# Retention layers: the next tile's rows transposed behind the gate projection, the gate function ahead of their scaling

## The reference

```
xn = layer_norm(x, ln1_scale, ln1_bias)
q, k, v = xpos(xn @ wq), xpos(xn @ wk), xn @ wv
heads = (q @ k.T * decay) @ v
y = group_norm(heads) * gn_scale + gn_bias
tmp = xn @ Wg;  swish = tmp * sigmoid(tmp)
x = swish * y @ Wo + x
```

## Time and profile before

| | |
|---|---|
| Time of the kernel before, median of 3 | 1639.94 us (1636.73 to 1643.91) |
| Time of the profiled execution | 1640.97 us |
| Its span, first to last instruction | 1639.2 us |
| PE busy | 1600.9 us, 98% |
| DVE busy | 1003.4 us, 61% |
| ACT busy | 848.5 us, 52% |
| Eight retention tiles of layer 0 | about 535 to 663 us |
| Eight retention tiles of layer 1 | about 850 to 986 us |

### The profile page before, as it was taken

One profiled execution on the slowest core, in us unless ns is written; L12 is line 12 of the kernel. 1 busy time (PEld: TensorE's weight loads), 2 busy tenths in 40 slices (PEclk: granted clock), 3 DMA queues, 4 the chain that ended last, 5 costly groups with the idle time before them and its releaser, 6 DMA issues.

```text
span 1639.2 us, 31503 instructions
## 1 busy us (share of the span) xinstructions
PE 1600.9 (98%) x12078; PEld 1344.9 (82%) x12078; DVE 1003.4 (61%) x2002; ACT 848.5 (52%) x1195; POOL 420.9 (26%) x358
## 2 busy tenths in 40 slices
PE   9999999999998999999999999999979999999997
PEld 8888888888887788888877888878878888888886
DVE  5334444444446777643366767444559999999994
ACT  4454444454445433453343334534337888788883
POOL 1333333333332544100005444000022112112111
PEclk8999999999999999999999999999989999999999
DMA  5110111111202100223241002234251555536612
GB/s 203 40 40 28 39 39 39 30 34 39 77 26 94 70 2 1 78 92 101 90 149 53 2 1 90 91 116 138 106 206 26 180 179 165 206 102 234 211 22 71
DMA packets 35840, 143.77 MB, mean 88 GB/s; under 512 B 4977, under 2 KB 5361, under 8 KB 28529
## 3 DMA queue, kind: packets, MB, share of 16 engines
q1 hardware_dynamic: 30592, 130.65, 22.7%
q0 software_dynamic: 5168, 12.06, 3.6%
HBM read 222.39 MB, written 12.85 MB: 144 GB/s over the span
## 4 chain that ended last, share of the span: by engine, by line
PE 59%; DVE 4%; DMA 2%; ACT 1%; issue 1%; POOL 0%; SPq 0%; DVEq 0%; POOLq 0%; ACTq 0%
PE bank L99 36%; PE bank L1664 10%; PE bank L2139 7%; PE bank L1555 2%; PE bank L2145 2%; PE bank L1568 1%; DVE e_w L2066 1%; DMA A<-xh_d,token 1%; PE bank L1648 1%; DMA out<-acc_d 0%; PE bank L1683 0%; DMA wraw<-in_wa 0%; DMA acc_d<-A,token 0%; DVE X L1530 0%; DVE fw L1360 0%
## 5 line engine op out<-in xcount | busy, mean ns | idle before, releaser
L2066 DVE TENSOR_TENSOR e_w<-e_raw,e_w 128x2048 fp32r<-128x2048 f32 x134 | 302.2, 2281 | 19.6 <-ACT e_w L1948 19.1
L1948 ACT ACTIVATE e_w<-e_raw 128x2048 fp32r<-128x2048 f32 x134 | 256.8, 1918 | 36.8 <-PE bank L2139 17.7
L99 PE MATMUL bank<-e_w,e_xT 128*128 128x512 f32 x1104 | 271.4, 395 | 0.0
L99 PEld LDWEIGHTS bank<-e_w,e_xT 128*128 128x128 f32 x1104 | 204.0, 188 | 41.3
L99 PE MATMUL bank<-ctx,wk 128*128 128x258 f32 x1536 | 191.8, 284 | 0.0
L1664 PE MATMUL bank<-fw,hh 128*128 128x512 f32 x768 | 186.2, 392 | 2.7 <-DVE hh L1482 2.7
L99 PE MATMUL bank<-x2T,fw 128*128 128x512 f32 x768 | 186.7, 392 | 0.0
L99 PEld LDWEIGHTS bank<-ctx,wk 128*128 128x128 f32 x1536 | 186.4, 192 | 0.2
L1664 PEld LDWEIGHTS bank<-fw,hh 128*128 128x128 f32 x768 | 144.5, 189 | 33.7 <-issue 2.2
L99 PEld LDWEIGHTS bank<-x2T,fw 128*128 128x128 f32 x768 | 143.5, 188 | 29.7
L622 DVE TENSOR_SCALAR_CACHE_REDUCE u<-bank,thr 128x257 f32<-128x257 f32 x128 | 54.5, 481 | 169.4 <-PE bank L826 169.4
(11 more groups left out here) (257 smaller groups left out, 2560.1 us busy)
## 6 DMA issues: line engine op xcount, KB each, us to landing
e_raw<-in_we SPq DMA_DIRECT2D x138, 1024.0 KB, 5.4
fraw<-in_wf SPq DMA_DIRECT2D x64, 512.0 KB, 3.6
ctxraw<-in_ctx SPq DMA_DIRECT2D x32, 514.0 KB, 3.5
wraw<-in_wa SPq DMA_DIRECT2D x20, 512.0 KB, 4.4
X<-in_x SPq DMA_DIRECT2D x4, 512.0 KB, 7.0
acc_d<-X SPq DMA_DIRECT2D x8, 256.0 KB, 4.0
xh_d<-A SPq DMA_DIRECT2D x8, 256.0 KB, 3.1
out<-acc_d SPq DMA_DIRECT2D x4, 512.0 KB, 5.8
```

What stands on the lines that cost most here:

```text
L99: last = nc.tensor.matmul(out, lhs(t, a), rhs(t, b), start=start and n == 0, stop=n == len(steps) - 1)
L1948: nc.scalar.activation(w[pos][:, 0, :, :], raw[pos][:, :, :], ACT.Copy).then_inc(m["w_hi"], 1)
L2066: nc.vector.tensor_tensor(w[pos][:, 1, :, :], raw[pos][:, :, :], r(w[pos][:, 0, :, :]), ALU.subtract).then_inc(m["w_lo"], 1)
```

## The change

On both engines one step moves to a later place in the same tile; nothing is added or taken away. It holds for tiles 1 to 6 of both layers, twelve tiles in all. Tile 0 had an order of its own already and keeps it, and tile 7 has no next tile.

```
# ACT
-                            if not (begin or end):
-                                norm_hi(n + 1, 1 - k)
                             act.wait_ge(m["v_ps"], n + 1)
...
                             nc.scalar.activation(sw[:, :], bank[3][:, :], ACT.Silu).then_inc(m["sw_ok"], 1)
+                            if not (begin or end):
+                                norm_hi(n + 1, 1 - k)
...
                             for j, turned in enumerate((qT, kT)):
# PE
-                            if not (begin or end):
-                                turn_next()
                             if not begin:
                                 pe.wait_ge(m["pf_ok"], 2 * n)
...
                             project(3, bank[3], k).then_inc(m["g_ps"], 1)
+                            if not (begin or end):
+                                turn_next()
                             for j in range(2):
                                 pe.wait_ge(m["qk_ok"], 4 * n + 2 * j + 2)
                                 turn(qk[:, j, :], bank[4 + j]).then_inc(m["qk_turned"], 1)
```

## The result

The changed kernel takes 1644.33 us in the median (1642.13 to 1647.72, 14 runs) against 1639.88 us before (1636.73 to 1643.91, 14 runs). The ratio is 1.0027, with a 95% interval of 1.0019 to 1.0034: 4.4 us more, between 3.1 and 5.6. The forecast was 1643.7, 3.8 more.

The account below looks back on a forecast made before the run. PE, busy 98% of the span, was taken as the bound. From the median of 1639.94 us, 3.4 for the two tiles 1 and 0.4 for ten others gave 1643.7 us (chance 0.83), range 1639.5 to 1648.0.

Parts of the forecast that it names:

- The stall of tile 1: Tile 1 of both layers: scores wait for ACT's later keys' copy, 1.62 to 1.77 us a layer, taken as 1.7.
- The step from the rounding to the queries' copy: ACT, tile 1: spacing not in the trace before, put between 0.49 (overlapping) and 0.64 us (its full length).
- the wait labelled issue: PE's 0.4 us wait at tile 1's scores: claimed to be for ACT's keys' copy, which ends 0.09 before the scores.
- PE's own cost: Moving four transposes into a longer row on PE: 0.04 us a tile, ends 0 and 0.06; 0.4 over ten tiles.
- The cover of the full tiles: Tiles 2 to 6: output projection hides ACT's delay, leaving 0.5 us in tile 2 and 1.0 in tiles 3 to 6.
- every tile pays: Rival, chance 0.04: scores wait for the keys' copy in tiles 2 to 6 too; 1660.3 us if cover failed altogether.
- What is late next: DVE: `norm_lo` waits for later rounded rows, takes about 0.69, ends by 589.9 in tile 3; residual at 590.92 isn't moved.
- The clock: Rival, chance 0.06: granted clock falls in tile 1, losing 1.7 us each time, 3.4 for two layers, giving 1647.1.
- The argument against it: Tile 0 of layer 0 has the same pattern, PE busy 1.09 of 2.00 us, and the clock stayed at 1.00.
- The text's own sign of being wrong: Tile 1 or 2: the prediction is wrong if the granted clock leaves 1.00 there.
- The profiled execution: The whole profiled run, 1640.97 us before with a span of 1639.2, would become 1644.8 with a span of 1643.0.
- Not slower: Rival, chance 0.07: tile 1's stall is absorbed later or the keys' copy goes ahead; 3.4 vanish, 1640.3 is left.

Follow-up runs that it names:

- tile1_old: Kernel after the change, but tile 1 of both layers in the order of before, so the move is in tiles 2 to 6 only; ratio 1.0001 to before.
- tile1_new: Kernel after the change, but with the move in tile 1 of both layers only; ratio 1.0024 to before.
- the doses: Kernel after the change with two or four extra Silu activations on ACT in tiles 1 to 6; ratios 1.0081 and 1.0183 to before.
- dose4: Kernel after the change with four extra Silu activations into an unread row, ahead of the real one, in tiles 1 to 6; ratio 1.0183 to before.
- before_b: Kernel before the change, run again unchanged for a third profile; ratio 0.9997 to before.
- after_a: Kernel after the change, run again unchanged for another profile; ratio 1.0032 to before.
- after_b: Kernel after the change, run again unchanged; ratio 1.0025 to before.
- after_c: Kernel after the change, run again unchanged; ratio 1.0035 to before.
- copies_first: Kernel after the change with transposes and scaling one place later still, behind queries and keys and behind their copies; ratio 1.0019 to before.
- pe_only: Kernel before with PE's half alone: next tile's transposes behind the gate projection, ACT's scaling still ahead of values' copy and Silu; ratio 1.0054 to before.

## Why the prediction was right, and where its terms were off

**The stall of tile 1.** Forecast 1.62 to 1.77 a layer, taken as 1.7; measured 16.88 - 15.23 = 1.65 and 16.88 - 15.21 = 1.67. The step from the rounding to the queries' copy, the unknown one, was 0.54, between the ends 0.49 and 0.64. PE waits in two pieces, 0.87 and 0.96, where the text had 0.9 and 1.2. It counted the whole 1.7 as idle time on top of the 0.40, but the waits grew only by 1.43: a row that used to reach into its follower now runs out first (1.04 us of the transposes of queries and keys, which before had given way after 0.87), and the transposes of `y` start 0.14 behind the end of the scaling (555.25 to 555.39), not at it. That the wait labelled issue is really ACT's was read from 0.09 us between two rows; `tile1_old` and `tile1_new` show that the loss sits there, and the doses that it follows ACT one for one (1.27 for 1.26).

**PE's own cost.** Forecast 0.04 for each of ten tiles, 0.4; measured from the scores of tile 1 to those of tile 7 0.15 and 0.13, 0.28 in all, most of it in tiles 2 and 3 (tile 2 of layer 0 by 0.07, a little over the 0.06 named as the limit). The four transposes cost 0.44 in their row (553.05 to 553.49), where 0.45 was forecast. The removal from one place and the addition at another nearly cancel: standing in one row with other transposes makes them no cheaper.

**The cover of the full tiles.** Forecast 0.5 us left in tile 2 and 1.0 in the others. After the change the keys' copy ends at 573.80 in tile 2, and the scores start at 574.56; less the 0.10 after a copy that is 0.66. In tile 3 it is 592.55 - 591.36 - 0.10 = 1.09. It held, so the rival "every tile pays" didn't come about, and `dose4` shows how much it costs once it does: 30 us.

**What is late next.** The step that was mis-sized is `norm_lo`, "takes about the same 0.69". It took 1.17 in tile 3 and 1.19 in tile 2, since it now runs beside POOL's scaling of the gate (the last section shows how), and the residual's idle time shrank to 0.63 and 0.18. The conclusion, that the residual isn't moved, was right with little to spare.

**The clock.** It had a chance of 0.06 as something that happens in both layers or not at all. It is neither: it happens in some executions. The price was right, 1.7 a fall against 1.6 measured (16.83 - 15.23 in `before_b`, 19.16 - 17.58 in `after_a`). The argument against it, that tile 0 has the same pattern and kept its clock, rested on one profile; in seven of fourteen it does not keep it. The text's own sign of being wrong, a granted clock below 1.00 in tile 1 or 2, is absent from the first profile and there in each of the three later ones: in `after_a` behind the stall, in `after_b` and `after_c` behind tile 0, where the kernel before has it too. So this argument was wrong, and leaving the clock out of the sum cost little only because a fall is small and doesn't come in each execution.

It goes some way to explain why the time rose by more than the 3.6 that every execution pays. With two falls in the ten layers that have the change's own stall, two layers cost another 2 x 0.2 x 1.6 = 0.6, which makes 4.2; by the one in eight of the kernel after itself it is 4.0. The mean granted clock, which is on record for every execution, points the same way: 0.9909 over the 35 of the kernel after, 0.9915 over 81 of the one before, and 0.0006 of 1640 us is 1.0 us, with an error of about 0.6. The four ratios lie between 4.1 and 5.7 us. That the forecast of 3.8 comes so near 4.4 is in part luck: its own terms were 0.2 too large together, which covered some of what it had left out. How often the clock falls behind tile 1 in this kernel, and so whether something small is still missing, stays open.

**The profiled execution.** For it the text had 1644.8 us and a span of 1643.0; it took 1647.72 and 1645.9, because of the long wait at the turn of the layers, which no term had. That the medians agree to 0.6 us doesn't test this: the wait is rare. Read alone, the first profile would have misled.

**Not slower.** Nothing later absorbed the stall. From the scores of tile 7 in layer 1 to the end it is 652.4 to 654.2 us in the four profiles after, and 653.6, 653.6 and 654.1 in those of before; that stretch scatters by more than the stall, so it is the ratios that show the loss is still there at the end.

## What to carry to other kernels

Before moving a step, ask in each place of the program what lies between it and the next wait: here ten tiles had a projection of 2.8 us as cover and two had none, and those two made the loss. A list written for the steady state is tested at its first tiles. Two orders that look different can have one bound by two ways, so cure both or neither; and a small stall on PE can be charged a second time by the clock, in some executions only, so one profile doesn't settle its price.

## What the runs showed of the hardware

The subtraction in `norm_lo`, 128x512 on DVE, took 0.68 to 0.69 us in tiles 1 to 6 of layer 0 before the change, and 1.13 to 1.28 after it. What differs is POOL. After the change it runs its scaling of the gate at that very time:

```profile
570.94 2.56 POOL L1090 TENSOR_TENSOR sws<-sw,gn_bc 128x512 f32<-128x512 f32 x2 [2.48 <-ACT sw L1178]
```

In `copies_first`, where `norm_lo` comes later (571.39, with POOL's scaling from 568.49 to 571.04), it takes 0.69 again, in all six tiles; so it does in `pe_only`, where it comes later too. In `tile1_new` it is 1.12 in tile 1 and 0.68 to 0.69 in the others. And before the change it took 1.10 in tile 0, while POOL was combining the rotated halves.

The rows read as a wait, not as a slower pace. In the rows above POOL's scaling ends at 570.94 + 2.56 = 573.50, and `norm_lo`, listed from 572.86, ends at 574.05, 0.55 later. Wherever it starts while POOL's instruction runs, in all 14 profiles, it ends 0.54 to 0.57 us behind the end of that instruction, whatever its own listed length (0.84 to 1.30). So its length tells how far POOL still had to go. The Trainium skill has a rule that fits ("SBUF — State Buffer", SBUF: two separate sides): DVE and GpSimd share a pair of ports, and of a DVE instruction with two SBUF inputs and a GpSimd instruction that reads SBUF, the one that starts first blocks the other to its end. `norm_lo` reads `xf` and `xn`, and the rows agree, with 0.55 us from POOL's end to its own. That it is the ports is the skill's word; the runs show only who waits for whom.

The granted clock fell behind pairs of gaps on PE with short products between them, in some executions and not in others of one and the same kernel: 7 times in 14 behind 1.2 to 1.3 and 0.7 us, 2 in 10 behind 0.9 and 1.0, and in none of 14 behind 0.6 and 0.7 to 0.8. It came back after about 3.4 us, and each fall cost some 1.6 us of work. Behind the wait of 3.08 us at the turn of the layers it stayed at 0.50 for some 6.8 us, and behind one of 2.40 at the same place in `pe_only` for 3.4.
